# Latent attention in a two-layer block: the output and its accumulation move to the second batch of weights, the maxima run ten pairs ahead, and TensorE sums all tiles of the last block

## The chip, the cores and the metric

The kernel runs on one core of one Trainium2 chip. The metric is the device time of one execution in microseconds (us). The matmuls named here run at full clock unless it is said otherwise.

## The reference

Two pre-norm layers follow one another on a sequence of S = 2048 rows of 128 numbers. Only the first attention is touched by the change. In it c_q and c_kv are 32 numbers wide, and there are H = 8 heads:

```python
c_q  = h @ W_DQ + b_DQ;   c_kv = h @ W_DKV + b_DKV
q = concat(c_q @ W_UQ + b_UQ, c_q @ W_QR + b_QR)      # per head, 128 + 32 wide
k = concat(c_kv @ W_UK + b_UK, h @ W_KR + b_KR)
attn = softmax(q @ k.T / sqrt(160), axis=-1)
o = attn @ (c_kv @ W_UV + b_UV)
x = x + o_of_all_heads @ W_O + b_O
```

After it come a feed-forward layer with two chosen experts (FFN 0), a second attention over 64 anchors, and a second layer of experts. They stay as they are.

## The kernel before

**Blocks, slots, tiles.** The attention is a loop over `NBLK` = 32 blocks `n`: head `n // 4`, and within a head 512 queries. A block has 16 tiles of 128 keys, two in each of `CPB` = 8 slots. For each tile TensorE (PE) forms transposed scores, keys by queries (`scores`, L1524), into one of three PSUM banks, and ScalarE (ACT) takes the exponential into `prob` (L655). The maximum that a softmax needs must be in the query columns before that, as one row of `q_cols`. It comes from a second pass over the same scores, with queries as rows: a row pair `lin` is two matmuls of 128 queries by 512 keys (`half_rows`, L1510), and VectorE (DVE) reduces each to one maximum per query (`chunk_max`, L1097). The eight pairs of a block make its 512 maxima. `minus_max` (L1105) folds them into `nmx`, and the queue SP sends `nmx` into its row of `q_cols` (L512). `scores` of the next block's first tile wait for that transfer.

**The lead.** Row pairs run ahead of the tiles. `row_pairs` (L196) says which pair goes with a slot: ten pairs ahead in block 0, a pair more in slot 2 of block 1 and of block 2, and twelve ahead from then on. Eight pairs before the loop and two more are done in the prologue.

**Weights and output.** `weighted` (L1568) multiplies `prob` with the values, four tiles side by side in the array: the first eight tiles in slot 6, the second eight in slot 1 of the next block. ACT copies the sum to `u_sb` (L628). Three blocks later, in slot 6, `output` (L1552) multiplies it with the head's folded output matrix `proj`, and DVE scales by the reciprocal of the softmax sums and adds into the rows `X` (`denominators` L1133, `accumulate` L1147). In block 30 the output of block 27 goes in slot 3.

**Softmax sums.** GpSimd (POOL) adds tiles in pairs (L941, L955, L962), a DMA from POOL's queue adds four more tiles in place (`late_sums`, L947, 1024 KB), and another joins the parts (`join_parts`, L969, 512 KB). PE then sums over partitions (`totals`, L1588, slot 6), ACT copies to `den_sb` (L636), and SP sends it to `den` (L501), 2 KB in words of 4 bytes, as `nmx` is. `denominators` waits for this transfer. SP's order in each block is L512 and then L501.

**PSUM banks.** Banks 3 to 6 go round among rows, keys, outputs and sums in the order of the program. `bank_read` makes a matmul wait until the item four before it in that order has been read, a maximum by DVE for a row. DVE, in one fixed order, is thus what PE waits for when rows come too fast.

**Keys.** `keys` (L1497, L1498) make 512 keys of the next head, and ACT and DVE split them (L621, L1083). `key_parts` says in which block.

**The end.** In block 31 POOL adds the first eight tiles in pairs (L941), and PE sums these parts (`first_totals`, L1609) and the last eight tiles themselves (`last_totals`, L1599). The layer norm of FFN 0 begins between these blocks: `ln0_stats`, `ln0_pool` (L339, L341), `ln0_norm` (`hn`, L359) and transposes on PE (L365).

## Time and profile before

| | us |
|---|---|
| median of 3 runs | 743.86 (743.17 to 744.91) |
| the profiled execution | 743.23 |
| its span in the profile | 741.4 |
| PE busy | 717.2 |
| DVE busy | 586.1 |
| POOL busy | 542.6 |
| ACT busy | 460.6 |

The span is what the profile sees of the execution. Some 1.8 us lie around it. Busy times of the engines overlap. A busy PE is one whose matmuls follow one another in the records, not one at its peak, so the table says which engine to look at and not how much can be gained. The blocks of the attention begin about 40 us from the start of the span and end near 498 us.

### The profile page before, as it was taken

How to read it: one execution, taken by the hardware profiler on the slowest of the kernel's cores; microseconds unless marked ns; L12 is line 12 of the kernel's file. 1: busy time of each engine (PE TensorE's matmuls, PEld its weight loads, DVE VectorE, ACT ScalarE, POOL GpSimd, SP SyncE). 2: the span in 40 equal slices, each digit the busy share in tenths (PEclk: the TensorE clock that was granted, in tenths of full speed). 3: DMA queues.
4: the chain of work that ended last, by engine and by line, in shares of the span. 5: the costliest groups of instructions: out<-in, count | busy, mean ns of one | idle time of the engine just before them, and what ended most of it. 6: DMA issues, size and time to landing. Idle time of an engine off the chain costs nothing.

```text
span 741.4 us, 12887 instructions
## 1 busy us (share of the span) xinstructions
PE 717.2 (97%) x4480; PEld 474.2 (64%) x4480; DVE 586.1 (79%) x1213; ACT 460.6 (62%) x1069; POOL 542.6 (73%) x444
## 2 busy tenths in 40 slices
PE   8999999999999999999999999989889999999997
PEld 7665556656656556556556555547656689778885
DVE  8878888888888888888888888764987736868885
ACT  4367757767767767766766666644787841455553
POOL 6468788888888888888888898623689861446764
PEclk9999999999999999999999999999999999999999
DMA  6223556646646647646646647004000000022431
GB/s 152 86 54 68 108 99 130 115 93 136 114 93 135 116 85 139 119 87 135 122 86 133 125 87 143 3 1 119 0 2 1 1 2 1 1 86 73 139 105 29
DMA packets 38853, 61.55 MB, mean 83 GB/s; under 512 B 14456, under 2 KB 23689, under 8 KB 34948
## 3 DMA queue, kind: packets, MB, share of 16 engines
q0 software_dynamic: 11936, 46.14, 31.9%
q1 hardware_dynamic: 25572, 14.47, 7.2%
q8 instruction: 36, 0.59, 0.3%
q10 hardware_dynamic: 1280, 0.12, 0.1%
q14 instruction: 29, 0.24, 0.1%
HBM read 13.35 MB, written 1.10 MB: 19 GB/s over the span
## 4 chain that ended last, share of the span: by engine, by line
PE 59%; DVE 22%; POOL 10%; issue 8%; ACT 1%; POOLq 0%; DVEq 0%
DVE mx L1097 16%; PE ps L1568 16%; PE ps L1524 9%; PE ps L1510 8%; PE ps L1552 5%; POOL hid_lo L1043 5%; PE ps L1939 4%; POOL nrm L1023 2%; PE ps L1588 2%; PE ps L1979 2%; PE ps L1981 2%; PE ps L1980 2%; POOL hid L1023 1%; PE ps L1497 1%; PE ps L1498 1%
## 5 line engine op out<-in xcount | busy, mean ns | idle before, releaser
L1097 DVE TENSOR_REDUCE mx<-ps 128x1 f32<-128x512 f32 x492 | 302.9, 682 | 66.5 <-PE ps L1510 66.5
L655 ACT ACTIVATE prob<-ps 128x512 f32<-128x512 f32 x512 | 262.3, 630 | 20.3 <-PE ps L1524 16.3
L1524 PE MATMUL ps<-q_cols,key 128*128 128x512 f32 x512 | 209.4, 412 | 0.7 <-ACT prob L655 0.7
L1510 PE MATMUL ps<-key,q_rows 128*128 128x512 f32 x512 | 207.6, 411 | 1.9 <-DVE key L1083 1.6
L1524 PEld LDWEIGHTS ps<-q_cols,key 128*128 128x128 f32 x512 | 95.5, 187 | 67.2 <-issue 33.3
L941 POOL TENSOR_TENSOR part<-prob 128x512 f32<-128x512 f32 x88 | 119.5, 1479 | 6.9 <-ACT prob L655 6.7
L1568 PE MATMUL ps<-prob,val 128*32 128x512 f32 x1024 | 124.2, 602 | 0.0
L955 POOL TENSOR_TENSOR pair<-prob 128x512 f32<-128x512 f32 x60 | 85.8, 1433 | 50.9 <-ACT prob L655 50.9
L1510 PEld LDWEIGHTS ps<-key,q_rows 128*128 128x128 f32 x512 | 95.6, 188 | 33.9 <-DVE mx L1097 17.8
L1043 POOL TENSOR_TENSOR hid_lo<-hid,hid_hi 128x512 fp32r<-128x512 f32 x44 | 61.4, 1407 | 38.8 <-ACT hid_hi L821 38.7
L636 ACT COPY den_sb<-ps 128x128 f32<-128x128 f32 x31 | 8.2, 266 | 90.0 <-PE ps L1588 90.0
L1568 PEld LDWEIGHTS ps<-prob,val 128*32 128x32 f32 x1024 | 26.9, 110 | 55.1 <-issue 50.0
L941 POOL TENSOR_TENSOR w_v<-prob 128x512 f32<-128x512 f32 x40 | 55.5, 1531 | 2.7 <-ACT prob L655 2.7
L962 POOL TENSOR_TENSOR part<-part,pair 128x1024 f32<-128x1024 f32 x20 | 47.6, 2380 | 0.0
L805 ACT ACTIVATE act_g<-ps 128x512 f32<-128x512 f32 x44 | 26.4, 600 | 33.1 <-PE ps L1981 32.8
L1147 DVE SCALAR_TENSOR_TENSOR X<-ps,rden,X 128x128 f32<-128x128 f32 x128 | 36.1, 344 | 7.3 <-PE ps L1552 4.1
L773 ACT ACTIVATE pT<-ps 128x128 f32<-128x128 f32 x128 | 33.6, 278 | 10.7 <-PE ps L1916 10.7
L1409 DVE TENSOR_TENSOR prod<-ps,act_g 128x512 f32<-128x512 f32 x44 | 30.1, 685 | 10.9 <-PE ps L1981 8.8
L1979 PE MATMUL ps<-hT_hi,w_hi 128*128 128x512 f32 x88 | 35.4, 403 | 0.0
L1981 PE MATMUL ps<-hT_lo,w_hi 128*128 128x512 f32 x88 | 34.6, 393 | 0.0
L1980 PE MATMUL ps<-hT_hi,w_lo 128*128 128x512 f32 x88 | 34.6, 393 | 0.0
L339 POOL TENSOR_SCALAR vare<-mv 128x4 f32<-128x4 f32 x12 | 4.7, 390 | 40.8 <-DVE mv L333 40.6
(294 smaller groups left out, 1227.6 us busy)
## 6 DMA issues: line engine op xcount, KB each, us to landing
part<-prob POOLq DMA_DIRECT2D x20, 1024.0 KB, 7.2
w_v<-prob POOLq DMA_DIRECT2D x10, 1024.0 KB, 7.2
part<-part POOLq DMA_DIRECT2D x19, 512.0 KB, 5.0
w_v<-w_v POOLq DMA_DIRECT2D x9, 512.0 KB, 5.1
g_all<-g_rows SPq DMA_DIRECT2D x9, 256.0 KB, 3.2
g_all<-g_rows SPq DMA_DIRECT2D x6, 224.0 KB, 3.0
X<-in_L_attn_h_t_dram SPq DMA_DIRECT2D x4, 256.0 KB, 4.2
out_dram<-X SPq DMA_DIRECT2D x4, 256.0 KB, 2.8
```

Source lines behind the costliest of these rows:

```text
L655: act.activation(prob[:, g % RING, :], ps[:, g % 3, :], ACT.Exp, scale=SCALE).then_inc(s_exp, 1)
L941: pool.tensor_tensor(part[n % 3][:, g, :], tiles(n, 2 * g, 1)[:, 0, :], tiles(n, 2 * g + 1, 1)[:, 0, :], ALU.add).then_inc(s_sum, 1)
L955: pool.tensor_tensor(pair[:, j, :], tiles(n, t, 1)[:, 0, :], tiles(n, t + 1, 1)[:, 0, :], ALU.add).then_inc(s_pair, 1)
L962: pool.tensor_tensor(p, p, pair[:, :, :], ALU.add).then_inc(s_sum, 1)
L1043: pool.tensor_tensor(hid_lo[:, n % 4, :], hid[:, n % 2, :], hid_hi[:, n % 4, :].bitcast(F32), ALU.subtract).then_inc(s_hlo, 1)
L1097: dve.tensor_reduce(mx[:, n % 2, c % TPB, at:at + 1], ps[:, BANK["rows", 2 * lin + j], :], AX.X, ALU.max).then_inc(s_mrd, 1)
L1510: pe.matmul(ps[:, BANK["rows", 2 * lin + j], :], q_rows[:, k, i * P:(i + 1) * P], key[:, h % KBUF, c0:c0 + BLK], start=True, stop=True).th ...
L1524: pe.matmul(ps[:, g % 3, :], key[:, n // NB % KBUF, t * P:(t + 1) * P], q_cols[:, n % NB, :], start=True, stop=True).then_inc(s_sc, 1)
L1568: last = pe.matmul(ps[C * x:C * (x + 1), U, :], val[:, t, :], prob[:, (NT * n + t) % RING, :], start=(t < NG), stop=(t >= NT - NG))
L1979: pe.matmul(out_ps, w[0], x_hi, start=start, stop=False)
L1980: pe.matmul(out_ps, w[1], x_hi, start=False, stop=False)
L1981: return pe.matmul(out_ps, w[0], x_lo, start=False, stop=stop)
```

## The change

The output of block n-3 and its accumulation move from slot 6 (slot 3 in block 30) to slot 1, from block 3 on. The maxima stay ten pairs ahead throughout, so that `minus_max` comes after slot 5 instead of slot 3, and block 30 has rows in slots 4 and 5 too. Key parts come one block later, always in slot 0. In block 31 PE sums all sixteen tiles: `last_totals(0)` and `last_totals(1)` take the place of POOL's four additions and of `first_totals`. In block 30 the statistics of the layer norm come ahead of DVE's two late sums instead of between them. All other code is the same, with line numbers up to 20 lower.

```diff
--- before.py
+++ after.py
@@ -190,21 +190,15 @@
         NG = P // C
         NW = NT // (2 * NG)
         LEAD = CPB + 2
-        AHEAD = 2
-        KLEAD = NB + 1
+        KLEAD = NB
 
         def row_pairs(n, slot):
 
-            first = CPB * n + slot + LEAD + min(max(n - 1, 0), AHEAD) + (1 if 1 <= n <= AHEAD and slot > 2 else 0)
-            count = 2 if 1 <= n <= AHEAD and slot == 2 else 1
-            return [lin for lin in range(first, first + count) if lin < NCHUNK]
+            lin = CPB * n + slot + LEAD
+            return [lin] if lin < NCHUNK else []
 
         def key_parts(n, slot):
 
-            if n == 2 and slot == 4:
-                return [n + KLEAD]
-            if n <= 2:
-                return [n + NB] if slot == 0 else []
             return [n + KLEAD] if slot == 0 and n + KLEAD < H * NB else []
         U = 7
         A_BANK = (4, 2)
@@ -260,7 +254,7 @@
                     todo.append(("queries", n + 2))
                 if slot == 5 and n == 0:
                     todo += [("folded", 0), ("folded", 1)]
-                if (slot == 6 and 3 <= n < NBLK - 2) or (slot == 3 and n == NBLK - 2):
+                if slot == 1 and 3 <= n < NBLK - 1:
                     todo.append(("out", n - 3))
                 if slot == 1 and n == NBLK - 2:
                     todo.append(("sums", n - 2))
@@ -969,14 +963,14 @@
                     pool.dma_start(part[n % 3][:, bass.ds(0, 2, step=2), :], part[n % 3][:, bass.ds(1, 2, step=2), :],
                                    accum_op=ALU.add).then_inc(s_join, 16)
 
-                for n in range(NBLK):
+                for n in range(NBLK - 1):
                     begin_sum(n, 0)
                     if n < 2:
                         columns(n + 2)
                     begin_sum(n, 1)
                     begin_sum(n, 2)
                     begin_sum(n, 3)
-                    if 1 <= n < NBLK - 1:
+                    if n >= 1:
                         add_pairs(n - 1)
                     if n < NBLK - 2:
                         late_sums(n)
@@ -1190,27 +1184,25 @@
                 for n in range(NBLK):
                     for slot in range(CPB):
                         lins = row_pairs(n, slot)
-                        for lin in lins[:1]:
+                        for lin in lins:
                             chunk_max(lin)
                         for e in key_parts(n, slot - 1):
                             keys_lo(e, BANK["keys", e])
                         if slot == 1 and n < 2:
                             queries_lo(n + 2, BANK["queries", n + 2])
-                        for lin in lins[1:]:
-                            chunk_max(lin)
                         if slot == 2 and n == 0:
                             values()
                         if CPB * (n + 2) - 1 in lins:
                             minus_max(n + 1)
-                        if (slot == 6 and 3 <= n < NBLK - 2) or (slot == 3 and n == NBLK - 2):
+                        if slot == 1 and 3 <= n < NBLK - 1:
                             denominators(n - 3)
                             accumulate(n - 3)
                         if slot == 6 and n == NBLK - 2:
                             denominators(n - 2)
                             accumulate(n - 2)
+                            ln0_stats(dve, 0)
+                        if n == NBLK - 2 and slot == 7:
                             late_sums(n, 0)
-                        if n == NBLK - 2 and slot == 7:
-                            ln0_stats(dve, 0)
                             late_sums(n, 1)
                         if n == NBLK - 1:
                             if slot == 0:
@@ -1592,21 +1584,14 @@
                 def last_totals(g):
 
                     n = NBLK - 1
-                    if g == 2:
+                    if g == 0:
                         bank_read(("sums", n))
                     pe.wait_ge(s_exp, NT * n + NG * (g + 1))
                     for x in range(NG):
                         last = pe.matmul(ps[C * x:C * (x + 1), BANK["sums", n], :], ones_v[:, :], prob[:, (NT * n + NG * g + x) % RING, :],
-                                         start=(g == 2), stop=(g == NG - 1))
+                                         start=(g == 0), stop=(g == NG - 1))
                     if g == NG - 1:
                         last.then_inc(s_ones, 1)
-
-                def first_totals():
-
-                    n = NBLK - 1
-                    pe.wait_ge(s_sum, begun(n))
-                    for g in range(NG):
-                        pe.matmul(ps[C * g:C * (g + 1), BANK["sums", n], :], ones_v[:, :], part[n % 3][:, g, :], start=False, stop=False)
 
                 def last_denominators():
 
@@ -1691,19 +1676,14 @@
                 pe.wait_ge(s_wal, 2)
                 for n in range(NBLK):
                     for slot in range(CPB):
-                        lins = row_pairs(n, slot)
                         scores(n, 2 * slot)
-                        for lin in lins[:1]:
+                        for lin in row_pairs(n, slot):
                             bank_read(("rows", 2 * lin))
                             half_rows(lin, 0)
                         scores(n, 2 * slot + 1)
-                        for lin in lins[:1]:
+                        for lin in row_pairs(n, slot):
                             bank_read(("rows", 2 * lin + 1))
                             half_rows(lin, 1)
-                        for lin in lins[1:]:
-                            for j in range(2):
-                                bank_read(("rows", 2 * lin + j))
-                                half_rows(lin, j)
                         for e in key_parts(n, slot):
                             bank_read(("keys", e))
                             keys(e, BANK["keys", e])
@@ -1718,7 +1698,7 @@
                             bank_read(("folded", 0))
                             bank_read(("folded", 1))
                             folded()
-                        if (slot == 6 and 3 <= n < NBLK - 2) or (slot == 3 and n == NBLK - 2):
+                        if slot == 1 and 3 <= n < NBLK - 1:
                             output(n - 3)
                         if slot == 6 and n == NBLK - 2:
                             output(n - 2)
@@ -1726,6 +1706,9 @@
                             weighted(n, 0)
                         if slot == 6 and 2 <= n < NBLK - 2:
                             totals(n - 2)
+                        if slot == 6 and n == NBLK - 1:
+                            last_totals(0)
+                            last_totals(1)
                         if slot == 1 and n >= 1:
                             weighted(n - 1, 1)
                         if slot == 1 and n >= NBLK - 2:
@@ -1743,7 +1726,6 @@
                                 bank_read(("norm", 1))
                                 ln0_pe(pe, 1, 4)
                                 weigh(n, range(2 * NG, 3 * NG))
-                                first_totals()
                 last_totals(3)
                 weigh(NBLK - 1, range(3 * NG, NT))
```

One block of DVE in the steady part of the attention, before. `mx` are maxima, `nmx` their negated fold, `key` the split keys, `rden` and `X` denominators and accumulation:

```order
L1097 TENSOR_REDUCE mx<-ps 128x1 x6
L1083 SCALAR_TENSOR_TENSOR key<-ps,kcol,key 128x512
L1097 TENSOR_REDUCE mx<-ps 128x1 x4
L1105 TENSOR_REDUCE nmx<-mx 128x4
L1097 TENSOR_REDUCE mx<-ps 128x1 x6
L1133 RECIPROCAL rden<-den 128x4
L1147 SCALAR_TENSOR_TENSOR X<-ps,rden,X 128x128 x4
```

The same block of DVE, changed:

```order
L1091 TENSOR_REDUCE mx<-ps 128x1 x8
L1099 TENSOR_REDUCE nmx<-mx 128x4
L1091 TENSOR_REDUCE mx<-ps 128x1 x8
L1077 SCALAR_TENSOR_TENSOR key<-ps,kcol,key 128x512
L1127 RECIPROCAL rden<-den 128x4
L1141 SCALAR_TENSOR_TENSOR X<-ps,rden,X 128x128 x4
```

`nmx` now stands behind eight maxima of the slots 2 to 5 instead of behind four, and the denominators and the accumulation stand ahead of those eight, behind the keys.

PE in slot 6 of a steady block, before, from its last row to the next scores (`proj` is the output, `prob,val` the weights, `part` or `w_v` with `ones_v` the sums):

```order
L1510 MATMUL ps<-key,q_rows 128x512
L1552 MATMUL ps<-proj,u_sb 128x128 x4
L1568 MATMUL ps<-prob,val 32x512 x8
L1588 MATMUL ps<-w_v,ones_v 32x128 x8
L1524 MATMUL ps<-q_cols,key 128x512
```

PE at the end of slot 1 of a steady block, changed:

```order
L1516 MATMUL ps<-q_cols,key 128x512
L1502 MATMUL ps<-key,q_rows 128x512
L1544 MATMUL ps<-proj,u_sb 128x128 x4
L1560 MATMUL ps<-prob,val 32x512 x8
L1516 MATMUL ps<-q_cols,key 128x512
```

The output has left slot 6, where weights and sums now follow the tenth row at once, and stands ahead of the second batch of weights.

PE in the last block, before, from the transposes of the layer norm (`hn`) on:

```order
L365 MATMUL ps<-ident,hn 128x128 x4
L1524 MATMUL ps<-q_cols,key 128x512 x4
L1568 MATMUL ps<-prob,val 32x512 x8
L1524 MATMUL ps<-q_cols,key 128x512 x2
L1552 MATMUL ps<-proj,u_sb 128x128 x4
L1599 MATMUL ps<-prob,ones_v 32x512 x4
L365 MATMUL ps<-ident,hn 128x128 x4
L1568 MATMUL ps<-prob,val 32x512 x4
L1609 MATMUL ps<-part,ones_v 32x512 x4
L1599 MATMUL ps<-prob,ones_v 32x512 x4
```

The same stretch, changed:

```order
L359 MATMUL ps<-ident,hn 128x128 x4
L1516 MATMUL ps<-q_cols,key 128x512 x4
L1560 MATMUL ps<-prob,val 32x512 x8
L1591 MATMUL ps<-prob,ones_v 32x512 x8
L1516 MATMUL ps<-q_cols,key 128x512 x2
L1544 MATMUL ps<-proj,u_sb 128x128 x4
L1591 MATMUL ps<-prob,ones_v 32x512 x4
L359 MATMUL ps<-ident,hn 128x128 x4
L1560 MATMUL ps<-prob,val 32x512 x4
L1591 MATMUL ps<-prob,ones_v 32x512 x4
```

Eight matmuls for the sums are new behind the weights of the first eight tiles, and the four on `part` are gone.

## Rows read from the trace of the kernel before

**Rows 1.** The page: busy us, share and instructions of PE

```profile
PE 717.2 (97%) x4480; PEld 474.2 (64%) x4480; DVE 586.1 (79%) x1213; ACT 460.6 (62%) x1069; POOL 542.6 (73%) x444
```

**Rows 2.** Windows: stretch and length, busy us, granted clock; blocks 1, 2, 3 to 29

```profile
59.41:72.70 13.29, 13.29 (x73) 6.97 (x69) 12.18 (x21) 9.94 (x18) 12.74 (x11) 1.00 0.34 69
72.70:88.47 15.77, 14.56 (x90) 7.89 (x86) 12.52 (x21) 10.54 (x20) 12.26 (x11) 1.00 0.61 117
88.47:464.80 376.33, 373.69 (x2458) 223.47 (x2455) 315.78 (x617) 256.18 (x510) 324.17 (x244) 1.00 0.59 114
```

**Rows 3.** Timeline of PE, 256 to 271 us: start, length, what

```profile
256.18 0.50 PE L1524 MATMUL ps<-q_cols,key 128*128 128x512 f32 x1
...
260.88 0.50 PE L1510 MATMUL ps<-key,q_rows 128*128 128x512 f32 x1
261.48 1.16 PE L1552 MATMUL ps<-proj,u_sb 128*128 128x128 f32 x8
262.57 1.92 PE L1568 MATMUL ps<-prob,val 128*32 128x512 f32 x16
...
264.86 0.50 PE L1524 MATMUL ps<-q_cols,key 128*128 128x512 f32 x1
...
268.31 1.92 PE L1568 MATMUL ps<-prob,val 128*32 128x512 f32 x16
270.16 0.50 PE L1524 MATMUL ps<-q_cols,key 128*128 128x512 f32 x1
```

**Rows 4.** Timeline of PE's weight loads: the wait ahead of the output, and its releaser

```profile
261.48 0.97 PEld L1552 LDWEIGHTS ps<-proj,u_sb 128*128 128x128 f32 x8 [0.41 <-DVE mx L1097]
```

**Rows 5.** Timeline of DVE in the same block

```profile
256.94 2.48 DVE L1097 TENSOR_REDUCE mx<-ps 128x1 f32<-128x512 f32 x4 [0.94 <-PE ps L1510]
259.46 0.17 DVE L1105 TENSOR_REDUCE nmx<-mx 128x4 fp32r<-128x16 f32 x1
259.55 3.67 DVE L1097 TENSOR_REDUCE mx<-ps 128x1 f32<-128x512 f32 x6
263.13 0.17 DVE L1133 RECIPROCAL rden<-den 128x4 f32<-128x4 f32 x1
263.41 1.12 DVE L1147 SCALAR_TENSOR_TENSOR X<-ps,rden,X 128x128 f32<-128x128 f32 x4
```

**Rows 6.** Timeline of SP, its two transfers in the same block

```profile
259.66 0.48 SPq L512 DMA_DIRECT2D q_cols<-nmx  x1
265.29 0.59 SPq L501 DMA_DIRECT2D den<-den_sb  x1
```

**Rows 7.** Timeline of POOL, its large transfer in the same block

```profile
262.79 0.89 POOL L947 DMA_DIRECT2D part<-prob  x1
```

**Rows 8.** DMA queues, issues: KB each, median us to landing

```profile
q_cols<-nmx SPq DMA_DIRECT2D x32, 2.0 KB, 1.9
```

**Rows 9.** DMA packets from 260.7 to 261.0 us: queue, packets, MB, share

```profile
q1 hardware_dynamic: 144, 0.00, 25.7%
```

**Rows 10.** DMA packets from 264.2 to 269.1 us, all there are

```profile
q0 software_dynamic: 128, 1.05, 103.8%
```

**Rows 11.** DMA packets from 269.1 to 269.5 us

```profile
q1 hardware_dynamic: 132, 0.00, 18.5%
```

**Rows 12.** DMA packets of SP's queue from 102.2 to 102.6 us, block 3

```profile
q1 hardware_dynamic: 33, 0.00, 4.9%
```

**Rows 13.** Timeline of DVE in block 31

```profile
478.97 5.13 DVE L359 TENSOR_SCALAR hn<-X,mv,rstd 128x128 f32<-128x128 f32 x4 [1.25 <-POOL rstd L341]
...
488.01 1.11 DVE L359 TENSOR_SCALAR hn<-X,mv,rstd 128x128 f32<-128x128 f32 x4 [1.47 <-POOL rstd L341]
```

**Rows 14.** Timeline of POOL in block 31

```profile
478.92 4.96 POOL L941 TENSOR_TENSOR part<-prob 128x512 f32<-128x512 f32 x4
```

**Rows 15.** Timeline of PE in block 31

```profile
484.25 0.63 PE L365 MATMUL ps<-ident,hn 128*128 128x128 f32 x4 [1.98 <-DVE hn L359]
...
486.52 2.88 PE L1568 MATMUL ps<-prob,val 128*32 128x512 f32 x16
```

**Rows 16.** Windows: 486 to 488 us, granted clock in the third column from the end

```profile
486.00:488.00 2.00, 2.00 (x9) 0.48 (x13) 0.54 (x6) 1.78 (x5) 1.26 (x2) 0.50 0.00 0
```

## The prediction

> **What bounds the kernel now.** First the page: PE is busy for 717.2 of 741.4 us [rows 1]. That is no proof of a full engine, so I next read the windows block by block [rows 2]: blocks 3 to 29 take 376.33 us, and a block with keys takes 13.98 us (270.16 - 256.18 [rows 3]). Then the timeline of one block, to see where PE waits. I count from s, the start of slot 2's first scores (s = 256.18), and call d the time from s to DVE's first maximum: 256.94, so d = 0.76 [rows 5]. From s PE issues ten scores and ten rows, the last at s+4.70, the output at s+5.30, the weights at s+6.39, slot 7 at s+8.68, the second weights at s+12.13, the next burst at s+13.98 [rows 3]. The output's loads waited 0.41 us for a maximum [rows 4]. DVE takes a maximum each 0.60 us (four in 2.48, six in 3.67, the last of each 0.68 long), and `nmx` puts 0.2 between the fourth and the fifth [rows 5]. In this burst PE is thus held by DVE, by the bank rule (a row waits for the sixth maximum, the output for the seventh). Outside it PE runs through. DVE's other work has room, and ACT and POOL are less busy than DVE and PE [rows 1].
>
> The DMA queues come last, because two small transfers move with the change. `nmx` goes out at s+3.48 [rows 6], its 144 packets run from 260.7 to 261.0 [rows 9], 1.1 us after the issue, and it lands 1.9 us after it [rows 8], so some 0.6 after its last packet. `den` goes out at s+9.11 [rows 6]. POOL's 1024 KB, issued at s+6.61 [rows 7], begin their packets at s+8.02. From 264.2 to 269.1 there are only those, eight for each of the 16 engines [rows 10]. The packets of `den` come from 269.1 on [rows 11], 3.8 us after its issue. So a small transfer that arrives behind the large one lands only at about s+13.3+0.55 = s+13.85. In block 3 a quarter of them came later still, near s+14.0 [rows 12]. Today nobody notices, for DVE reads `den` in slot 6 of the next block.
>
> **The change, a steady block.** The output leaves the tail of the burst. The tenth row waits for the sixth maximum, which is no longer behind `nmx`: s+0.76+5x0.60+0.68 = s+4.45, and PE alone would be there at s+4.5. The weights follow at s+4.8 (no wait) to s+5.1 (0.60 later, as today's output). I take 4.95. Then come weights and sums 2.29 (8.68 - 6.39), slots 7 to 1 with the keys 3.45, the output 1.0 (1.09 less one switch), and the second weights 1.85, in all **13.5 us** against 13.98. The engine is not asked for less: only the wait goes.
>
> *What is late next.* DVE now needs `den` in slot 1. The copy follows the sums at s+7.3 and the issue at s+7.6 (today 265.29 is 0.43 after 264.86), with packets ready at s+8.7. POOL's transfer keeps its place: POOL had idle time before the additions that lead to it, and now gets more, so its packets still begin at s+8.02. `den` then lands at s+13.85. Reciprocal and accumulation take 0.28 + 1.04, with 0.05 to wake [rows 5]: DVE is free at s+15.22. If the block took 13.5, that is d = 1.72 in the next one, 1.0 later than today. With such a lag the weights start at s+d+4.2 and the block takes d + 12.7. So two lags in a row sum to 15.22 - 12.7 = 2.5: a block with 1.7 is followed by one with 0.8, and the mean block is 12.7 + 1.25 = **13.97**. The wait removed is given back by the wait for `den`. A lag is not damped by this law, so every second block keeps the high one.
>
> *The shift row.* `nmx` now stands behind eight maxima: its issue is at s+d+5.1 (259.66 - 256.94 = 2.72, and four maxima more). With d = 0.76 its packets start at s+7.0, ahead of POOL's at s+8.02, and land at s+7.8, when scores need it at s+4.95+2.29+1.0 = s+8.2. With d = 1.72 they start at s+7.9, and with the 0.2 to 0.6 by which `den` scatters [rows 12] at s+8.1 and more. The limit is d = 1.8. Beyond it the row waits out POOL's transfer and lands at s+14.0. Scores stand until s+14.1, and the next burst begins 3.45 - 1.0 + 1.0 + 1.85 = 5.3 later, at s+19.4. PE has then stood still for over 4 us. After 1.98 us of standing in block 31 the granted clock fell to 0.50, the 1.2 GHz level [rows 15, 16], and sixteen matmul records took 2.88 instead of 1.92. I add 1.0 per such stop (bounds 0 and 2). That block takes 20.4 and resets d to 0.76, so that the next is 13.5 and the one after it at the edge again. A pair with a stop takes 33.9, without 27.95: **5.95 per stop**, at most 14 stops (blocks 3 to 29, every second one). Which of the edge cases fall over the limit I can't read within 0.1 us; I take half, **7 stops**.
>
> A rule speaks otherwise. The Trainium skill, page "DMA: Bandwidth & Descriptors", section "Queues, rings and completion order", says that each engine goes round-robin between the queue rows that have work, at packet granularity. If its packet were what the profile counts as one, `den` would get its turn after one of eight and nothing would be late: the third rival, and 726 us. If its packet is the "9-17 descriptors typical" of the same sentence, the eight are one turn, and that is what the rows show. I go by the rows.
>
> **The change, elsewhere.** Block 1 has one pair less and no nmx delay: 13.29 becomes 13.5 - 1.0 (no output) - 0.44 (no sums) = 12.1, a gain of 1.2. Blocks 2 to 29, 15.77 + 376.33 = 392.1 [rows 2], become 28 x 13.97 = 391.2. Keys stay 28 in number (block 27 gets one, block 2 has one less), three of the blocks end without keys, worth 0.7, and block 30's extra sums add 0.9: 391.4, a gain of 0.7. The extra pair and the late keys that made block 2 long go, but the output that block 3 now has in slot 1 falls into this stretch. Block 30 gets four rows (4 x 0.23 = 0.9) and loses one output (1.0): nothing. SP's and POOL's orders are the same but for the end. In block 31 POOL's four additions (4.96 us [rows 14]) go. They ran while DVE's four `hn` took 5.13 instead of the 1.11 of the same form later [rows 13], so PE's wait of 1.98 [rows 15] goes, and the clock fall behind it, 1.0, too. What is late next there these rows don't show; the bounds below take it in. The statistics ahead of the late sums in block 30 cost nothing, since PE asks for those sums only in slot 4 of block 31. Two groups of four sums come, one goes, each 0.87 (half of the 1.74 of the sixteen weight records, 262.57 up to the sums): +0.9. The end gains 2.1 (bounds 0 and 3).
>
> **The sum**, against the profiled execution of 743.23 (span 741.4 and 1.8 around it; 0.6 under the median): 743.2 - 1.2 - 0.7 - 2.1 = 739.2 without stops, + 7 x 5.95 = 41.7, gives **781 us**.
>
> **The rivals.**
> 1. *Only `den` is late, the shift row always gets through.* For it: d = 1.72 is under 1.8. Against: one scattered `den` is over it, and the mean lag does not shrink. Time 739, with the landing 0.6 later (28 x 0.3) 748, with the end and burst at their best 735. This is the case on the other side, faster than before; it decides at d = 1.8.
> 2. *A stop in every second block.* 739.2 + 14 x 5.95 = 822. It takes only 0.1 us more of lag than I have. It is the upper end of my own case.
> 3. *`den` gets in between POOL's packets.* Then neither lag nor stop: 28 x 13.5 + 0.2 = 378.2, a gain of 13.9, and 743.2 - 13.9 - 1.2 - 2.1 = 726. Against it are rows 10 and 11.
>
> **The numbers.** Stops in some or most of the second blocks (one to fourteen, 745 to 826): 0.68, and beyond 826, with a slower clock after each, 0.04. Lag alone 0.20, of which 0.13 faster, 0.05 the same, 0.02 slower. Free transfers 0.08. A measurement here can tell some 0.2%, 1.5 us. Faster is 0.13 + 0.08 = 0.21, and a little of the first case where a good end outweighs a single stop, 0.22. Same 0.05, slower 0.73. The range 737 to 826 leaves out the free case, the lowest third of the lag case and the excess above, 0.19 in all.
>
> **What would show it.** `den`'s reciprocal should be ended by DMA, not by DVE's own order, and the first maximum after it alternate between 0.8 and 1.7 us after slot 2's scores. Some scores of slot 0 (L1516) should wait 4 to 5 us for `q_cols`, whose landing is then about 7 us instead of 1.9. A clock below 1.00 should show behind them. `hn` of block 31 should take 1.1 us, and no wait stand ahead of its transposes. I am wrong if all landings of `nmx` stay at 1.9 (rival 1 or 3), and if the reciprocal never waits (rival 3).

## The result, and the profile after

The changed kernel takes **804.72 us** (median; 803.57, 804.40 and 805.04, and one execution at 823.12) against 743.86: ratio 1.0812, 95% interval 1.0791 to 1.0833 (without the execution at 823.12). Run again later (last experiment) it gave six times between 783.2 and 836.5. The forecast was 781, range 737 to 826. The profiled execution took 804.40, its span 802.6.

The page, with the lines that answer to [rows 1] and the new waits: busy us, then for PE's scores the idle time and its releaser.

```profile
PE 739.4 (92%) x4488; PEld 486.5 (61%) x4488; DVE 585.4 (73%) x1213; ACT 470.0 (59%) x1069; POOL 539.2 (67%) x440
...
PE 56%; DMA 15%; DVE 11%; POOL 9%; issue 6%; ACT 1%; POOLq 0%; DVEq 0%
...
L1516 PE MATMUL ps<-q_cols,key 128*128 128x512 f32 x512 | 217.6, 428 | 42.8 <-DMA q_cols<-nmx 42.2
```

The waits by engine: total us, times, longest.

```profile
PE ps L1516 <- DMA q_cols<-nmx: 42.2, 9, 5.9
```

and all of DVE's reciprocals (L1127), from the view of that line:

```profile
  DMA den<-den_sb: 29.0, 19
```

No other engine got slower by itself: DVE and POOL are busy as long as before, and ACT's exponentials take 618 ns in the mean for 630. What is new are two waits for SP's small transfers, 15% of the chain.

Windows, columns as in [rows 2]: block 1 with what leads to it, blocks 2 to 29, blocks 30 and 31, and everything behind them.

```profile
58.00:71.60 13.60, 13.60 (x82) 7.11 (x74) 12.44 (x21) 9.84 (x20) 11.60 (x10) 1.00 0.24 50
71.60:524.38 452.78, 407.90 (x2550) 240.72 (x2546) 330.58 (x639) 277.00 (x530) 337.07 (x254) 0.95 0.52 99
524.38:555.64 31.26, 30.64 (x258) 17.43 (x255) 21.91 (x70) 18.94 (x42) 12.80 (x10) 1.00 0.01 2
555.64:802.60 246.96, 234.97 (x1274) 183.45 (x1272) 173.65 (x381) 135.94 (x427) 144.33 (x113) 0.97 0.14 42
```

Blocks 2 to 29 took 392.1 and now take 452.8: +60.7. Block 2 starts 1.1 earlier (71.60 for 72.70), blocks 30 and 31 are 3.2 shorter (31.26 for 464.80 to 499.27, 34.47), and the unchanged code behind them is 4.8 longer (it was 242.1). Together +61.2, which is the difference of the two profiled executions (804.40 - 743.23).

**A block with a stop.** Block 11 begins at s = 211.75. DVE's timeline, then SP's and POOL's, then PE's, and last the window with the granted clock:

```profile
212.22 0.18 DVE L1127 RECIPROCAL rden<-den 128x4 f32<-128x4 f32 x1 [1.62 <-DMA den<-den_sb]
212.51 1.13 DVE L1141 SCALAR_TENSOR_TENSOR X<-ps,rden,X 128x128 f32<-128x128 f32 x4
213.55 4.87 DVE L1091 TENSOR_REDUCE mx<-ps 128x1 f32<-128x512 f32 x8
218.45 0.17 DVE L1099 TENSOR_REDUCE nmx<-mx 128x4 fp32r<-128x16 f32 x1
```

```profile
218.65 0.48 SPq L506 DMA_DIRECT2D q_cols<-nmx  x1
220.42 0.59 SPq L495 DMA_DIRECT2D den<-den_sb  x1
```

```profile
218.34 0.89 POOL L941 DMA_DIRECT2D w_v<-prob  x1
```

```profile
220.81 0.40 PE L1502 MATMUL ps<-key,q_rows 128*128 128x512 f32 x1
225.62 0.63 PE L1516 MATMUL ps<-q_cols,key 128*128 128x512 f32 x1 [4.41 <-DMA q_cols<-nmx]
226.04 0.63 PE L1502 MATMUL ps<-key,q_rows 128*128 128x512 f32 x1
...
229.03 0.50 PE L1516 MATMUL ps<-q_cols,key 128*128 128x512 f32 x1
229.37 0.40 PE L1502 MATMUL ps<-key,q_rows 128*128 128x512 f32 x1
...
232.44 0.50 PE L1516 MATMUL ps<-q_cols,key 128*128 128x512 f32 x1
```

```profile
227.00:229.00 2.00, 2.00 (x6) 1.55 (x5) 1.09 (x2) 1.12 (x2) 1.12 (x1) 0.50 0.36 64
```

DVE waits for `den`, so d = 1.80 (213.55 - 211.75), and the shift row is issued at s+6.90, 0.3 after POOL's transfer. It lands 6.92 later, PE stands 4.41, and then its matmuls follow each other in 0.43 instead of 0.23: the granted clock is 0.50, the 1.2 GHz level, until 229.0. From the first scores behind the stop to the next burst it is 6.82 us, where block 4, without a stop, needs 5.21 (114.07 to 119.28): 1.6 for the clock. The block takes 20.69.

All 28 blocks in that way: blocks 3, 9, 11, 13, 15, 17, 19, 21 and 23 have a stop and take 20.51 to 23.11, 21.34 in the mean. Each is followed by one of 13.48, with d back at 0.77. Blocks 5 to 8 and 25 to 29 have a lag and no stop: d is 1.59, 0.94, 1.62, 1.08 in blocks 5 to 8. The latest shift row that got through went out at s+6.72 (block 7), the earliest that did not at s+6.86 (block 21).

**What the packets do.** In block 3 the row goes out at s+8.02 (93.10), when POOL's packets already run. The packets from 93.0 to 98.0, then from 98.0 to 98.5:

```profile
q0 software_dynamic: 128, 1.05, 101.7%
```

```profile
q1 hardware_dynamic: 276, 0.00, 34.0%
```

This is [rows 10, 11] again: 128 large ones, then everything of SP. In block 11 the row is only a little late. The packets from 220.2 to 224.7, and from 224.7 to 225.45:

```profile
q0 software_dynamic: 112, 0.92, 101.0%
q1 hardware_dynamic: 112, 0.00, 3.6%
```

```profile
q0 software_dynamic: 54, 0.08, 60.3%
q1 hardware_dynamic: 159, 0.00, 13.3%
```

Here they take turns, one small packet for each large one. That does not help: the row has nine packets for each of the 16 engines (144), POOL's transfer eight, of which seven still run beside the row's (112 and 112), in 4.5 us.

### The profile page after: what moved, and what is told of

It reads as the page before. It is cut to its first block, busy times and chain, and to the rows that moved or that the text cites. A ratio compares the mean times of both kernels' runs of the same rounds, so it can differ in the third digit from the quotient of the medians.

```text
span 802.6 us, 12898 instructions
## 1 busy us (share of the span) xinstructions
PE 739.4 (92%) x4488; PEld 486.5 (61%) x4488; DVE 585.4 (73%) x1213; ACT 470.0 (59%) x1069; POOL 539.2 (67%) x440
## 4 chain that ended last, share of the span: by engine, by line
PE 56%; DMA 15%; DVE 11%; POOL 9%; issue 6%; ACT 1%; POOLq 0%; DVEq 0%
PE ps L1516 12%; PE ps L1502 11%; PE ps L1560 11%; DMA q_cols<-nmx 8%; DMA den<-den_sb 7%; DVE mx L1091 5%; POOL hid_lo L1037 4%; PE ps L1921 4%; PE ps L1544 3%; POOL nrm L1017 2%; PE ps L1961 2%; PE ps L1963 1%; PE ps L1962 1%; PE ps L1580 1%; DVE X L1141 1%
## 5 line engine op out<-in xcount | busy, mean ns | idle before, releaser
L649 ACT ACTIVATE prob<-ps 128x512 f32<-128x512 f32 x512 | 271.9, 618 | 67.0 <-PE ps L1516 62.5
L1516 PE MATMUL ps<-q_cols,key 128*128 128x512 f32 x512 | 217.6, 428 | 42.8 <-DMA q_cols<-nmx 42.2
L1502 PE MATMUL ps<-key,q_rows 128*128 128x512 f32 x512 | 219.5, 433 | 3.5 <-DVE X L1141 2.4
L1516 PEld LDWEIGHTS ps<-q_cols,key 128*128 128x128 f32 x512 | 99.4, 195 | 105.7 <-DMA q_cols<-nmx 46.7
L935 POOL TENSOR_TENSOR part<-prob 128x512 f32<-128x512 f32 x84 | 111.9, 1418 | 68.9 <-ACT prob L649 68.7
L1502 PEld LDWEIGHTS ps<-key,q_rows 128*128 128x128 f32 x512 | 99.7, 196 | 54.0 <-DVE mx L1091 29.8
L622 ACT COPY u_sb<-ps 128x512 f32<-128x512 f32 x22 | 12.9, 587 | 42.8 <-PE ps L1560 42.8
```

The lines of the kernel that those rows point to most:

```text
L649: act.activation(prob[:, g % RING, :], ps[:, g % 3, :], ACT.Exp, scale=SCALE).then_inc(s_exp, 1)
L935: pool.tensor_tensor(part[n % 3][:, g, :], tiles(n, 2 * g, 1)[:, 0, :], tiles(n, 2 * g + 1, 1)[:, 0, :], ALU.add).then_inc(s_sum, 1)
L1502: pe.matmul(ps[:, BANK["rows", 2 * lin + j], :], q_rows[:, k, i * P:(i + 1) * P], key[:, h % KBUF, c0:c0 + BLK], start=True, stop=True).th ...
L1516: pe.matmul(ps[:, g % 3, :], key[:, n // NB % KBUF, t * P:(t + 1) * P], q_cols[:, n % NB, :], start=True, stop=True).then_inc(s_sc, 1)
```

## The experiments

All times are beside runs of the kernel before on the same chip: 743.5 us for experiments 1 to 4, 743.2 for 5 to 7 and the second run of 2, 743.6 for 8 to 10, 743.4 for 11. Of the longer edits the main lines are shown.

**1. Only the end.** The kernel before, with the sums of block 31 all made on TensorE:

```diff
-                for n in range(NBLK):
+                for n in range(NBLK - 1):
                     begin_sum(n, 0)
...
+                        if slot == 6 and n == NBLK - 1:
+                            last_totals(0)
+                            last_totals(1)
```

> The kernel before with the last block's edit alone: POOL's four additions and the four sums of parts go, eight sums of tiles come in slot 6. My sum gives -2.1 us: hn of block 31 takes 1.1 instead of 5.1 us and the wait of 1.98 us and the clock fall behind it go. In the changed kernel the granted clock falls near the start of FFN 0 instead, where the same code takes 4.8 us longer than before. If that fall follows from the last block's edit, this kernel shows it too and is 1 to 3 us slower than before; if it follows from the stops, it doesn't, and the kernel is 2 to 3 us faster.

Measured: 741.12, ratio 0.9977 (0.9965 to 0.9989), -2.4. As the prediction had it, the first four `hn` of block 31 take 1.12 instead of [rows 13]'s 5.13, and no wait stands ahead of the transposes:

```profile
479.02 1.12 DVE L359 TENSOR_SCALAR hn<-X,mv,rstd 128x128 f32<-128x128 f32 x4 [1.25 <-POOL rstd L341]
```

The fall of the clock near the start of FFN 0, which the change showed, isn't in this profile. Another is, 44 us behind block 31 (granted 0.84 from 540 to 550, after ten in which PE was busy for 7.30), in a kernel without any stop.

**2. Maxima ten ahead, output where it was.**

```diff
-                        if slot == 1 and 3 <= n < NBLK - 1:
+                        if (slot == 6 and 3 <= n < NBLK - 2) or (slot == 3 and n == NBLK - 2):
```

in its three places, from the changed kernel. I call this kernel 2.

> The changed kernel, but output and accumulation back in slot 6 (slot 3 in block 30); maxima ten pairs ahead and the new last block stay. Queue theory: den is read late as before, DVE has no lag (0.76), the shift row is issued at about s+5.9 and its packets are gone at s+7.3, ahead of POOL's at s+8.0: no stops, block 13.7 to 13.98 us, total 732 to 744. Rival of the lead (maxima ten ahead put the shift row too late by their own place): stops of over 4 us in blocks here too, 780 or more.

Measured: 733.49, ratio 0.9861 (0.9846 to 0.9875), **faster than before**, and 732.41 (0.9864) when it ran again:

> The kernel that was fastest so far (change but the output in slot 6 as before), run again beside the others on one chip: 733.5 again (731 to 738). If the sums-first kernel comes to 725 to 729.5, moving the output to slot 1 is worth 28 x 0.30 = 8.4 us once den is early, by the blocks of 13.48 against 13.78; if it comes to 733 or more, slot 1 has nothing that slot 6 hasn't.

In the profile of the second run blocks 3 to 26 take 13.77 and no block waits for a transfer: `den` is read in slot 6, and the shift row goes out at s+5.87. The weight loads of the output in block 10 (s = 180.45) wait for the same 0.41 as in [rows 4], but at s+5.09 and not s+5.30, since `nmx` is no longer ahead of the maximum they wait for:

```profile
185.54 0.97 PEld L1544 LDWEIGHTS ps<-proj,u_sb 128*128 128x128 f32 x8 [0.41 <-DVE mx L1091]
```

That is 0.21 for each of the 23 blocks that have keys in both kernels (3 to 25), 4.8 us. Block 2, without its extra pair and late keys, takes 12.51 where it took 15.77 (3.3). So two of the change's parts gain about 10 us, and the third, the output in slot 1, loses some 70.

**3. Output in slot 1, maxima still twelve ahead** (with the extra pairs and the key parts of the kernel before), so that `nmx` stays behind four maxima.

```diff
+        AHEAD = 2
...
+            first = CPB * n + slot + LEAD + min(max(n - 1, 0), AHEAD) + (1 if 1 <= n <= AHEAD and slot > 2 else 0)
```

> The changed kernel, but with the maxima twelve pairs ahead as before; output and accumulation stay in slot 1. Queue theory (the small transfers wait out POOL's 1024 KB one): den is late as in the changed kernel, so DVE's reciprocal waits up to 2 us, but the shift row is issued some 2.4 us earlier and always lands after 1.9 us, so PE never stands for it: 740 to 747 us. Rival (it is the accumulation in slot 1 itself that holds DVE and PE, whatever the lead): stops of 4 to 6 us remain and the time stays near 800. Rival of the lead (the ten-pair lead alone does it, den costs nothing): no wait for den on the path, 726 to 733.

Measured: 746.75, ratio 1.0052 (1.0033 to 1.0070). DVE waits for `den` 27 times (28.1 us), d goes to and fro (0.77 and 1.75, in blocks 9 to 16 all near 1.1, then again from 0.76 to 2.12), blocks 3 to 25 take 13.67 to 14.66, and there is no stop, for the shift row goes out by s+4.8. This is the lag alone: rival 1, worth nothing or a little less. The stops need the row behind eight maxima as well.

**4. POOL's transfer held** until the shift row has landed.

```diff
+                    if n >= 2:
+                        pool.wait_ge(s_shift, 16 * (n + 2))
                     pool.dma_start(part[n % 3], tiles(n, 2 * NG, NG), accum_op=ALU.add).then_inc(s_late, 16)
```

> The changed kernel, but from block 2 on POOL issues its 1024 KB transfer only once the shift row of the next block has landed (about s+7.8 instead of s+6.6). Queue theory: the shift row is always ahead, and den, issued at s+7.6 with packets at s+8.7, gets ahead of packets that now begin at s+9.2, so neither lag nor stop: all blocks 13.5 us, and with the end 726 to 733. If den still falls behind: no stops but a lag, 740 to 748. Rival (DVE's order or PE's banks are the cause, not the queue): near 800 as the changed kernel, or slower by the held transfer.

Measured: 742.47, ratio 0.9989 (0.9962 to 1.0015). PE never stands for the row, not even in block 5, where d is 2.74 and the row goes out at s+7.84, far beyond the limit. So it is POOL's transfer that stops it, and not the lag. The hope for blocks of 13.5 throughout (726 to 733) failed, for a held transfer comes late: blocks 4 and 5 take 14.93 and 15.45, the quiet ones 13.48. In block 5 `den` is late behind it. In block 4 it is not (d is 0.76): there ACT waits 1.39 for the transfer of the block before, which still reads `prob`, and PE 1.22 for ACT. ACT's wait, and POOL's in the same block:

```profile
102.84 2.56 ACT L649 ACTIVATE prob<-ps 128x512 f32<-128x512 f32 x5 [1.39 <-DMA part<-prob]
```

```profile
107.62 0.90 POOL L943 DMA_DIRECT2D part<-prob  x1 [2.05 <-DMA q_cols<-nmx]
```

**5. The sums ahead of the weights** in slot 6, so that `den` is early.

```diff
-                        if slot == 6:
-                            weighted(n, 0)
                         if slot == 6 and 2 <= n < NBLK - 2:
                             totals(n - 2)
+                        if slot == 6:
+                            weighted(n, 0)
```

> The change, with the sums of slot 6 (whose result is copied and sent out as den) ahead of the weights of that slot instead of behind them: 1.0 us earlier on TensorE, so that den is issued about s+6.2 instead of s+7.6 and its packets are ready at s+7.3, ahead of POOL's 1024 KB at s+8.02. Nothing else is moved. Theory 1 (den behind POOL's transfer starts everything, and the shift row is only late because den is): den lands at s+8.2, DVE never waits for it in slot 1, d stays 0.76, the shift row goes out at s+5.9 and no scores stand. All blocks from 3 on take 13.48; against the 743.5 of the kernel before: 28 x 13.48 = 377.4 for 392.1 is -14.7, block 1 -1.1, the end -3.2, in all 724.5, and up to 729.5 if the clock falls in FFN 0 as in the changed kernel. Rival (the shift row is late by itself, since it now stands behind eight maxima): the stops stay, about 800. Rival (weights 1.0 us later hold up something else, a ring place or a bank): no stops, blocks of about 14, 740.

Measured: 729.79, ratio 0.9833 (0.9814 to 0.9852). 75 us less than the change, by the order of two calls. SP's timeline in block 4 (s = 98.93), and the packets from 105.75 to 107.0:

```profile
104.81 0.48 SPq L506 DMA_DIRECT2D q_cols<-nmx  x1
105.39 0.59 SPq L495 DMA_DIRECT2D den<-den_sb  x1
```

```profile
q1 hardware_dynamic: 276, 0.00, 10.9%
```

POOL's begin at 107.0. No lag (d = 0.77) and no stop in any block, so in the changed kernel both begin with a late `den`. The size was missed: blocks take 13.64, not 13.48, and the time is 729.8, not 724.5. The sums now meet the bank rule that the weights had been free of:

```profile
104.03 0.38 PEld L1580 LDWEIGHTS ps<-w_v,ones_v 128*32 128x32 f32 x16 [0.41 <-DVE mx L1091]
```

**6. POOL's transfer in two halves.**

```diff
-                    pool.dma_start(part[n % 3], tiles(n, 2 * NG, NG), accum_op=ALU.add).then_inc(s_late, 16)
+                    for g in (0, 2):
+                        pool.dma_start(part[n % 3][:, g:g + 2, :], tiles(n, 2 * NG + g, 2), accum_op=ALU.add).then_inc(s_late, 16)
```

(and its two waits count to 32 a block).

> The change, with POOL's 1024 KB addition of each block as two of 512 KB, four packets for each of the 16 DMA engines instead of eight; den and the shift row keep their places. Theory 1a (a whole transfer is one turn of an engine, and another queue gets in behind it): den, ready at s+8.7, gets in behind the first half, at about s+10.5 to 11, lands about s+11.5, DVE is free at s+12.9 and never late for the next burst at s+13.48: no lag, no stop, 725 to 730, if POOL can pay for a second issue (0.9 us a block; POOL is busy for 12.0 of 13.5 us a block in the changed kernel) and otherwise up to 745. Theory 1b (both halves are queued on the engine before den arrives and drain as one): nothing changes, some 800, or more with the second issue. The landing of a late shift row tells it too: 5.8 to 8.4 us under 1b, under 4 us under 1a.

Measured: 753.59, four times from 739.7 to 755.8. Between the two theories: the row behaves nearly as 1a has it, `den` as 1b. The late shift row of block 8 lands after 4.4 us (1a had under 4) and not 7, and PE stands 1.87 and goes on at full clock. (Behind a stand of 1.96 in block 6 the clock fell, and that block took 18.19, block 8 16.79.) In block 8 these are the packets from 167.2 to 168.2 and from 168.2 to 168.45:

```profile
q0 software_dynamic: 48, 0.20, 108.2%
q1 hardware_dynamic: 48, 0.00, 7.2%
```

```profile
q0 software_dynamic: 31, 0.06, 132.2%
q1 hardware_dynamic: 96, 0.00, 27.6%
```

The row takes turns while the first half runs, and all that is left of it goes where the halves meet. `den`, 1.8 later on the same queue, comes behind the second half as before, so the lags stay.

**7. Both of these.**

> Both together: sums ahead of the weights of slot 6, and POOL's addition in two halves. If den is early by the order alone, the halves have nothing left to give: the time of the run with the sums first, plus what a second issue costs POOL (0.9 us a block; nothing if POOL has room, up to 25 us if POOL bounds the block). Rival: den is still late in some blocks with the sums first, then the halves take these away and this is the fastest of all.

Measured: 730.77, ratio 0.9829 (0.9807 to 0.9852), the same as 5 within the intervals. With `den` early the halves have nothing to give, and POOL had room for the second issue.

**8. The output in slot 7**, behind the burst and the sums.

```diff
-                        if slot == 1 and 3 <= n < NBLK - 1:
+                        if (slot == 7 and 3 <= n < NBLK - 2) or (slot == 3 and n == NBLK - 2):
```

(in the same three places as in 2).

> The change with output and accumulation of block n-3 in slot 7 of block n, behind DVE's burst and behind the sums, instead of in slot 1. Theory 1 (the gain of the change is to take the output out of the burst, its cost is to ask for den too early): den is asked for a whole block after it landed, the shift row goes out at s+5.9, and the burst has no output in it. Blocks of 13.48, no DMA wait in any: 743.3 - 14.7 - 1.1 - 3.2 = 724.3, with 1 to 5 us more if the clock falls in FFN 0: 724 to 729, ahead of the sums-first kernel (729.8, blocks of 13.64) by 0.16 x 28 = 4.5. Rival (an output behind the burst meets another wait: its bank has just held row maxima or the sums, or DVE's accumulation of 1.3 us delays the maxima of slot 7 and the key): blocks of 13.6 to 13.8, 729 to 733.

Measured: **725.22, ratio 0.9754 (0.9738 to 0.9771)**, the fastest of all, 18 us under the kernel before. Blocks 3 to 26 take 13.53 to 13.67, and from block 2 to block 27 PE has no idle time and the full clock:

```profile
71.73:422.43 350.70, 350.70 (x2335) 213.24 (x2331) 304.79 (x592) 251.04 (x493) 313.99 (x237) 1.00 0.62 119
```

**9 and 10. The shift row alone, later by one and by two maxima.** From kernel 2, where `den` is not asked for early, `nmx` behind one or both maxima of slot 6. The second:

```diff
-                        if CPB * (n + 2) - 1 in lins:
+                        if slot == 6 and n < NBLK - 1:
                             minus_max(n + 1)
```

> From the kernel with the maxima ten ahead and the output in slot 6 (732.4 us, no DMA wait, blocks of 13.77), nmx computed one maximum later on DVE, between the two of slot 6: the shift row is issued at s+6.47 instead of s+5.87, its packets are ready at s+7.6, ahead of POOL's at s+7.95. den is not asked for early here, so only the shift row is tried. Theory 1 (a limit at s+6.7 to 6.9, where POOL's packets begin 1.1 later): nothing changes, 732 to 734. Rival (a later row costs in proportion, it is late by degrees): 0.6 us a block, up to 750.

> The same with nmx two maxima later, behind both of slot 6: issued at s+7.07, packets ready at s+8.2, behind the start of POOL's. Theory 1: the row waits out the 1024 KB in every block from 2 to 29, lands about s+14.0 instead of s+9.0, slot 0's scores (due at s+9.5) stand 4.5 us, the clock falls behind each stop for 1.8 us more, so a block takes 13.77 + 6.3 = 20.1, and the kernel 732.4 + 28 x 6.3 = 909 (890 to 930). Rival (packets interleave, or the lag of den was needed too): landing 1.9 us, s+9.0, still ahead of the scores: 732 to 734. Rival (stops but no clock fall): 732.4 + 28 x 4.5 = 858.

Measured for one: 738.75, ratio 0.9942 (0.9920 to 0.9963). The blocks are as short as without it (13.78, row out at s+6.34). The 6 us over the expected 732 to 734 are lost ahead of block 3, which I had not looked at: PE waits 2.76 for a row at 57.2, and 0.26 and 1.22 in blocks 1 and 2, and from 57 to 60 us its granted clock is 0.50. In block 2 the row went out at s+6.34 like the others and still landed only after 3.3. For two: 929.47, ratio 1.2508 (1.2477 to 1.2540). The row goes out at s+6.95 and stops PE in all 28 blocks, for 4.1 to 5.8 us; the expected 909 was 20 us short, for a stop costs 6.8 and not 6.3, and the blocks ahead of block 2 lose time as well. With no lag of `den` at all, 0.6 us more on the row's way turn nothing into 190 us. Its median landing, and PE's idle time over the whole kernel:

```profile
q_cols<-nmx SPq DMA_DIRECT2D x32, 2.0 KB, 7.1
```

```profile
L1516 PE MATMUL ps<-q_cols,key 128*128 128x512 f32 x512 | 237.4, 467 | 136.2 <-DMA q_cols<-nmx 135.6
```

Blocks 2 to 28 took 20.54 in the mean, for 13.78 or a little less, so nearly 7 a stop: 4.7 of standing (135.6, less 3.5 ahead of block 2, over 28) and some 2 of slow clock (212.86 to 219.31 behind the stop of block 8, 6.45, for 4.26 in kernel 2; 2.2 there).

**11. The changed kernel once more.**

> The changed kernel itself, unaltered, run once more with a profile, for the 4.8 us that it lost in FFN 0 at a granted clock of 0.69 and 0.80 (560 to 580 us of its first profile), though the code is that of the kernel before. Theory A (the fall belongs to this kernel: TensorE reaches FFN 0 without a gap, since the wait of block 31 is gone): the fall stands at the same place of the profile, and every run takes 803 to 806. Theory B (it falls in some executions and not in others): the runs spread over some 5 us, 799 to 805, and this profile may be without it, with 242 us from block 31's end instead of 247. The nine stops should stand either way, give or take two: each pair with one costs 6.9, so a profile with seven would be at 790, with eleven at 818.

Measured: 783.23, 792.47, 813.66, 816.12, 817.04 (the profiled one) and 836.54. The kernel before stayed between 741.97 and 745.37 beside it. These six are one cloud, so I give no ratio and read the one that has a profile. It has eleven stops:

```profile
PE ps L1516 <- DMA q_cols<-nmx: 50.6, 11, 5.8
```

In blocks 5 and 29, which had passed with the row at s+6.69 and s+6.63, it went out at s+6.84 and s+6.86 and stopped. The clock did not fall in FFN 0, and from block 31's end it is 242.14 again:

```profile
573.06:815.20 242.14, 230.18 (x1274) 180.30 (x1272) 173.60 (x381) 136.10 (x427) 144.47 (x113) 1.00 0.14 43
```

So theory B for the clock, with far more spread than it allowed. Between the two profiles it is the number of rows over the limit that differs most. The other five executions have no profile; at 6.9 a stop on some 738 without any, 783 and 837 would be 6 to 7 and about 14 stops, which is an estimate of mine and not shown.

## Why the prediction was right, and where it was short

- **P_min 13.5**: 13.48 in every block without lag. Right.
- **The lag law**, block = d + 12.7 and d + d' = 2.5: blocks 5 to 7 took 14.29, 13.65 and 14.32 with d of 1.59, 0.94 and 1.62, so 12.70 and 2.53 to 2.56. Right there, but not everywhere: behind d = 1.08 in block 8 came 2.35 in block 9 (the law gives 1.4), and behind 0.76 in block 2 came 2.93 in block 3. In these two `den` was read at s+14.81 and s+15.05 and not at s+13.85. I can't say what made it so late. Experiment 3 is this lag alone, 746.8 where rival 1 had 739 to 748, but slower than before, not faster.
- **"The limit is d = 1.8"**: it lies between 1.62 and 1.76, row out between s+6.72 and s+6.86. I had it 0.04 to 0.18 too high.
- **"Seven stops"** is the first term that was too small: nine, and eleven in the second profile. Behind a resetting block `den` was mostly read 0.1 to 0.5 later than s+13.85 (in block 11 at 212.22, s+13.96 from block 10's start; in block 17 at s+14.32; in blocks 5 and 25 at s+13.72), so that d was mostly 1.76 to 2.16 and not 1.72, against a limit some 0.1 lower. Seven was half of fourteen and not worked out, so that it came near nine is in part luck. The prediction said that this can't be read within 0.1 us. It couldn't, and the kernel itself doesn't hold it within 0.1 from one execution to the next.
- **"5.95 per stop"** is the second: a stop's block took 21.34 and not 20.4, and a pair 34.82 against 27.95, 6.9. Of the 0.94, 0.65 lies behind the start of the scores (6.95 in the mean for my 5.3 + 1.0; against the 5.21 of block 4 the clock costs 1.7 and not 1.0), and 0.3 is scores that start at s+14.4 in the mean and not at s+14.1. In three of the nine blocks (9, 13, 19) the wait was over 5 us. In block 13, from 260.4 to 261.2, three of SP's packets come as late as that, among 80 of POOL's next transfer. The view doesn't tell whether they are the row's or `den`'s:

```profile
q0 software_dynamic: 80, 0.16, 109.9%
q1 hardware_dynamic: 3, 0.00, 0.3%
```

- **How the row waits.** The step said that it waits out POOL's transfer, and that the third rival's rule had the packets take turns. The time came out by the step, but the packets do take turns when the row is only a little late (112 and 112), and none does when it is later (block 3). The Trainium skill, page "DMA: Bandwidth & Descriptors", section "Queues, rings and completion order", has each engine go round-robin between queue rows, packet by packet. If its packet is what the profile counts as one, the 112 and 112 agree, and the 128 large ones in a row of [rows 10] and of block 3 do not. My use of the rule in the third rival was the mistake: I let the small transfer need one turn, and it needs nine, so that it would be late by that rule too.
- **Block 1, -1.2**: -1.1. **The end, -2.1**: -3.2, a little outside its bounds of 0 and 3; alone (experiment 1) it is -2.4.
- **Not in the prediction**: 4.8 us in FFN 0, where the clock fell in code that nothing touches (the granted clock is the third column from the end):

```profile
560.00:570.00 10.00, 9.75 (x53) 7.35 (x51) 3.35 (x16) 3.20 (x8) 0.00 (x0) 0.69 0.45 123
570.00:580.00 10.00, 9.36 (x43) 6.01 (x43) 4.08 (x17) 3.40 (x7) 3.96 (x5) 0.80 0.01 3
```

Against the prediction's 781.0: two more stops and a dearer pair (9 x 6.87 = 61.8 for 41.7) +20.1, the clock +4.8, the end -1.1, makes 804.8 for 804.40.

What the experiments show as cause is the chain `den`, lag, row, stop: take the first away (5) and all goes; move the row alone (10) and the stops come without the lag; take POOL's transfer from the row's way (4) and they go with the lag still there. What sets which blocks fall over the limit stays open, and so does what makes the clock fall in FFN 0.

## What to carry to other kernels

Before a read is moved ahead, ask when its data lands, and behind which large transfer it was queued while nobody minded; a small transfer has to be issued well before the large one's packets start (here the last row that got through was 1.3 us ahead of them, the first that didn't 1.16), and where the two take turns it pays a large packet for each of its own per engine, nine here for only 2 KB. Where two waits feed each other through such a limit, count what lies 0.1 us from it as open: here the same kernel ran in 783 or in 837 us. The gain of taking work out of a burst was real, and moving the work later, to where its data had long landed (slot 7), kept it.

## What the runs showed that I had not expected

- How soon the packets of two queues take turns hangs on how late the second comes. With the row out at s+6.90 (block 11) one round of large packets went first, at s+7.26 (block 17) five, at s+8.02 (block 3) all eight; `den`, later still, got none in ([rows 10]). I can't say why.
- A row that misses the limit can land up to 8.4 us after its issue instead of 1.9 (block 9), when POOL's next transfer, 512 KB, already runs. That it waits for this one too isn't shown: in block 9 the last packets of SP's queue ran before 190.0, and the scores started at 191.24.
- Behind the attention TensorE's granted clock fell to the 1.2 GHz level for 3 to 10 us in eight of the fourteen profiles here, and not in that of the kernel before. In some of them PE had stood for about 2 us, in others it hadn't: in kernel 2's first profile (738.33, its other runs 732.04 to 734.06) from 500 to 510 us, while its second profile has no such stretch there:

```profile
500.00:510.00 10.00, 10.00 (x38) 6.17 (x38) 1.51 (x4) 2.81 (x7) 0.97 (x1) 0.60 0.00 1
```

It was 0.50 from 498 to 507 us. PE had been busy for 9.75 of the 10 us before, so here no standing of some us went ahead of the fall.
